# A graph network's edge matrix with a column per node, built from tiles of five nodes; first pass written out

## Reference, cut to what matters

```python
def gin_conv(x, W_a, b_a, W_b, b_b):                     # layer 0, twice
    agg = segment_sum(x[src], dst, N)
    return relu((agg + x) @ W_a + b_a) @ W_b + b_b
...
def gcn(x):                                              # layer 1, two hops
    x = relu(x); deg = segment_sum(1, dst, N); d = rsqrt(max(deg, 1))
    for _ in range(2): x = segment_sum(x[src] * d[src] * d[dst], dst, N)
    return x
...
# layer 2: three spline convolutions (each edge mixes 8 of 64 matrices by its
#   attributes), mean over a node's edges, leaky relu, batch norm
# layer 3: attention with 4 heads over the same edges (softmax by segment)
```

## Time and profile before

| | |
|---|---|
| median of three runs | 13,891.47 us (13,890.89, 13,891.47, 13,902.91) |
| span of the profiled execution | 13,892.9 us (it has no time of its own beside the span) |
| busy PE, PEld | 8,563.9 us (62%), 5,687.6 us (41%) |
| busy DVE, ACT, POOL | 7,277.8 (52%), 2,041.8 (15%), 9,883.4 (71%) |
| setup | 0 to 84.87 us |
| gin1, its node phase | 84.87 to 1,763.59, to 1,909.63 |
| gin2, what stands between | to 3,217.70, to 3,325.42 |
| gcn1, what stands between | to 4,134.10, to 4,184.33 |
| gcn2 | to 4,994.07 |
| spline passes and attention | to 13,892.9 |

### The profile page before, as it was taken

The page is one execution under the profiler, slowest core; times in us unless marked ns, Lnnn a source line. Parts: engine busy times, 40 slices in busy tenths (PEclk is TensorE's granted clock), DMA queues, the critical chain, the costliest instruction groups (busy, mean ns, idle before and its releaser), DMA issues.

```text
span 13892.9 us, 190634 instructions
## 1 busy us (share of the span) xinstructions
PE 8563.9 (62%) x45374; PEld 5687.6 (41%) x45374; DVE 7277.8 (52%) x21844; ACT 2041.8 (15%) x1668; POOL 9883.4 (71%) x10259
## 2 busy tenths in 40 slices
PE   5666667776877866666667666667666660033315
PEld 2333323333444445545445545545455540032305
DVE  5555522223333366666666666666666661245637
ACT  5666710000000001111111111111111110000000
POOL 7777747775767757777767777767777765777772
PEclk8887868888989977778878887778778775566657
DMA  4544523344767730000010000010000002122212
GB/s 122 154 143 145 150 70 102 103 107 115 215 181 215 214 75 13 13 13 13 13 16 13 13 13 13 13 16 13 13 13 13 13 12 38 32 57 57 57 39 47
DMA packets 1111612, 930.87 MB, mean 67 GB/s; under 512 B 312738, under 2 KB 1066308, under 8 KB 1111061
## 3 DMA queue, kind: packets, MB, share of 16 engines
q10 hardware_dynamic: 641040, 670.91, 15.8%
q0 software_dynamic: 325632, 190.97, 8.8%
q1 hardware_dynamic: 144518, 64.66, 2.1%
HBM read 718.69 MB, written 207.12 MB: 67 GB/s over the span
## 4 chain that ended last, share of the span: by engine, by line
POOL 62%; issue 22%; PE 7%; DVE 4%; ACT 2%; DVEq 1%; DMA 1%; ACTq 0%; SPq 0%; POOLq 0%
POOL work L802 62%; PE ps L910 2%; PE ps L925 2%; ACT nodes L1289 2%; DVEq L1740 1%; PE ps L1111 1%; PE ps L898 1%; PE ps L1028 0%; DVE big L1750 0%; DVE big L1823 0%; DVE nodes L1762 0%; PE ps L1122 0%; PE ps L1139 0%; DVE nodes L1758 0%; ACTq L1413 0%
## 5 line engine op out<-in xcount | busy, mean ns | idle before, releaser
L802 POOL DMA_INDIRECT work<-tab_sp,nodes x4992 | 4725.1, 947 | 1735.6 <-issue 1520.1
L1006 PE MATMUL ps<-work 128*128 128x192 f32 x9984 | 2671.8, 411 | 1905.9 <-DVE work L1672 1850.4
L1006 PEld LDWEIGHTS ps<-work 128*128 128x128 f32 x9984 | 1992.9, 232 | 2482.0 <-issue 1440.7
L1921 DVE TENSOR_TENSOR work<-work,ps 128x192 f32 x4992 | 1748.3, 350 | 719.9 <-PE ps L1006 372.6
L802 POOL DMA_INDIRECT work<-tab_att,nodes x1664 | 1603.9, 964 | 628.3 <-issue 628.3
L991 PE MATMUL ps<-work,wk 128*32 128x144 f32 x10080 | 1760.9, 327 | 2.3 <-DVE work L1921 2.3
L925 PE MATMUL ps<-nodes,work 128*96 128x480 fp8e4 (+1 forms) x6664 | 1613.9, 400 | 64.7 <-DVEq L1872 59.2
L802 POOL DMA_INDIRECT work<-in_x,idx x1248 | 1302.8, 1044 | 416.8 <-issue 375.5
L1750 DVE TENSOR_TENSOR big<-big,ps 33x12 f32 (+2 forms) x3520 | 554.8, 158 | 1939.5 <-PE ps L898 1214.5
L1672 DVE TENSOR_TENSOR work<-work,ps 128x512 f32<-128x512 f32 x1248 | 856.0, 686 | 1333.5 <-DMA work<-tab_sp,nodes 1317.9
L1331 ACT ACTIVATE work<-zero 128x2496 f32<-128x2496 f32 x318 | 725.4, 2282 | 5453.1 <-PE ps L991 5448.4
(11 more groups left out here) (241 smaller groups left out, 6117.1 us busy)
## 6 DMA issues: line engine op xcount, KB each, us to landing
nodes<-counts_d ACTq DMA_DIRECT2D x612, 660.0 KB
counts_d<-nodes ACTq DMA_DIRECT2D x130, 1188.0 KB
work<-tab_sp,nodes POOLq DMA_INDIRECT x4992, 2.4
work<-counts_d ACTq DMA_DIRECT2D x117, 528.0 KB
work<-edge_rows SPq DMA_DIRECT2D x112, 320.0 KB
edge_rows<-work ACTq DMA_DIRECT2D x104, 320.0 KB, 2.2
work<-tab_att,nodes POOLq DMA_INDIRECT x1664
work<-in_x,idx POOLq DMA_INDIRECT x1248
```

Source lines behind the costliest of these rows:

```text
L802: pool.indirect_dma_start(out=rows(p, r)[:, t, 0:ROW[p]], out_offset=None, in_=TABLE[p], in_offset=bass.IndirectOffsetOnAxis(ap=place, axi ...
L1006: last = nc.tensor.matmul(moment_place(t), u0[:, s % 2, t % SUB, :], vb[:, t % AHEAD, :, :].rearrange("p k j -> p (k j)"), start=True, sto ...
L1921: v.tensor_tensor(to, to, got, ALU.add).then_inc(mom_added.sem, 1)
```

## The change

The matrix gets a column per node in place of a 12-wide window per tile. Five successive target nodes (KN) are a tile, so a block of counts is 128 x 490 (98 x 5), and the five columns of one tile touch those of the next: a pair of 40 tiles is 200 nodes, 2,000 tiles (KT) in 50 pairs are 10,000 nodes. Where a tile's edges begin isn't known before: in the setup DVE counts, for each of 16 groups of 128 five-node tiles, how many edge tiles begin below its first node; POOL gathers those edge tiles' targets (16 gathers) and, once DVE has counted on, sources and targets of 128 edges a tile (32 gathers); DVE works out codes, an edge that doesn't belong to the five nodes gets a code that matches nothing, PE turns codes and low parts, ACT copies them out. The test now compares 14 neighbours instead of 10, in a ring of 8, and asks that no five nodes have too many edges.

Dense are now the first 9,800, 8,800, 10,000 and 10,000 nodes. Near halves fall to 24, 32, 22 and 22 (384, 512, 352 and 352 gathers); at the seam a 32-tile stretch has its edges to dense nodes hidden while a pass runs (`cut_off`).

In gin1, PE builds two tiles a step, one product of 490 columns each into a PSUM bank of its own (a ring of three steps; the code ring goes from 4 to 8), ACT evicts the two in one instruction of 980 elements, 5 adjacent bytes at a time 200 bytes apart, and the dense product takes the pair's counts straight from the staging buffer, 98 products of 200 columns, while the next pair is built. The store of a whole pair (2.5 MB) is issued by SP. All of gin1 is written out on PE, DVE and ACT, in turns of 80 tiles with one near half each. The later passes are written out as well: units of 400 columns, pieces through a ring of six, 22 units in gin2 and 25 in each gcn pass; DVE adds a finished unit in one instruction at a fixed place. x is turned in the setup beside DVE's counts.

The diff, cut to its core:

```diff
-DT = 1040
-DENSE = {"gin1": 416, "gin2": 640, "gcn1": DT, "gcn2": DT}
-UNIT = {"gin1": 32, "gin2": 40, "gcn1": 40, "gcn2": 40}
-PIECES = {"gin1": 2, "gin2": 2, "gcn1": 3, "gcn2": 3}
+KN = 5
+KSTEP = 2
+PAIR = 40
+PN = PAIR * KN
+PAIRS = 50
...
+NEAR_HALVES = {"gin1": 24, "gin2": 32, "gcn1": 22, "gcn2": 22}
+DENSE = {p: ET - G * n for p, n in NEAR_HALVES.items()}
+DENSE_NODES = {"gin1": 9800, "gin2": 8800, "gcn1": PAIRS * PN, "gcn2": PAIRS * PN}
+UNIT = 2
+UN = UNIT * PN
...
+PIECES = 6
+CODE_RING = 8
...
+DIST = 14
+PAIR_RING = 8
...
+            def store_pairs():
+                with sp.Fori(0, PAIRS // 2) as i:
+                    for h in range(2):
+                        j = 2 * i + h
+                        sp.wait_ge(evicted.sem, evicted.done("gin1", STEPS * j + (STEPS - 1)))
+                        sp.dma_start(counts_d[bass.ds(j, 1), :, :, :].rearrange("g c p n -> p (g c) n"),
+                                     staged_out[:, h, :].rearrange("p (c n) -> p c n", c=NCH)).then_inc(counts_out[h], 16)
...
+            hold(pool, "pool", firsts_known, 1)
+            for c in range(KCOLS):
+                pool.indirect_dma_start(
+                    out=dst_rows[:, c, :], out_offset=None, in_=single_dst,
+                    in_offset=bass.IndirectOffsetOnAxis(ap=tile_edge[:, c:c + 1], axis=0),
+                ).then_inc(dst_rows_in, 16)
+            hold(pool, "pool", edges_known, 2)
+            for c in range(KCOLS):
+                for to, single, at_ in ((edge_src, single_src, first_edge), (edge_dst, single_dst, first_ext)):
+                    pool.indirect_dma_start(
...
-            def build_counts(n, b):
+            def build_counts(n, b, step, ring):
...
-                for q in range(3):
-                    w = CODES // 3
-                    last = nc.tensor.matmul(ps[:, 3 * (b % 2) + q, 0:w], lo_oh[:, (b // SUB) % 2, b % SUB, :],
-                                            code_oh[:, b % 4, q * w:(q + 1) * w], start=True, stop=True)
-                last.then_inc(built.sem, 1)
+                for q in range(KSTEP):
+                    hold(pe, "pe", code_made.sem, code_made.done("gin1", n + q))
+                    if q == 0:
+                        pe.wait_ge(evicted.sem, evicted.done("gin1", step - 3))
+                    nc.tensor.matmul(ps[:, 2 * ring + q, 0:KC], lo_oh[:, (b // SUB) % 2, (b + q) % SUB, :],
+                                     code_oh[:, (b + q) % CODE_RING, :], start=True, stop=True).then_inc(built.sem, 1)
...
+                def dense(j, h, e):
+                    blocks_ = dense_blocks(e)
+                    if e == DENSE_FROM:
+                        hold(pe, "pe", evicted.sem, evicted.done(p, STEPS * j + (STEPS - 1)))
+                        hold(pe, "pe", unit_added.sem, unit_added.done(p, j - 2))
+                        pe.sem_inc(asked_pe, 1)
+                    for t in blocks_:
+                        last = nc.tensor.matmul(ps[0:SPLIT1, 7, 256 * h:256 * h + PN], parts1[:, t, 0:SPLIT1],
+                                                staged_counts[:, h, t * PN:(t + 1) * PN], start=(t == 0),
+                                                stop=(t == NT - 1))
...
+                    for x in range(2):
+                        for e in range(STEPS):
+                            f = STEPS * x + e
+                            build_counts(TURN_K * turn + KSTEP * f, KSTEP * f, 2 * STEPS * turn + f,
+                                         (2 * STEPS * phase + f) % 3)
+                            if k is not None and f in NEAR_AT:
+                                near(k, y, NEAR_AT.index(f), i)
+                            if k is not None or x == 1:
+                                dense(2 * turn + (x - 1), 1 - x, e)
...
+            def evict_counts():
...
+                            if e == 0:
+                                hold(act, "act", counts_out[x], 16 * turn + 16)
+                                hold(act, "act", pair_used.sem, pair_used.done("gin1", 2 * turn + (x - 2)))
+                            act.wait_ge(built.sem, built.done("gin1", TURN_K * turn + (KSTEP * f + KSTEP - 1)))
+                            nc.scalar.activation(out_[:, KSTEP * e:KSTEP * (e + 1), :, :],
+                                                 ps[:, 2 * ring:2 * ring + KSTEP, 0:KC].rearrange("p q (m w) -> p q m w", w=KN),
+                                                 ACT.Copy, saturate=False).then_inc(evicted.sem, 1)
...
+                def add_pair(j, h, n_added):
...
+                    to = acc[0:SPLIT1, bass.ds(j * PN, PN)]
+                    v.tensor_tensor(to, to, ps[0:SPLIT1, 7, 256 * h:256 * h + PN], ALU.add).then_inc(unit_added.sem, 1)
...
+                def add_unit(u, n_added):
...
+                    to = acc[0:m, u * UN:(u + 1) * UN]
+                    v.tensor_tensor(to, to, ps[0:m, u % 4, 0:UN], ALU.add).then_inc(unit_added.sem, 1)
...
+            for c in range(KCOLS):
+                link(v.tensor_scalar(pen_f[:, 0:SEEN], first_target.bitcast(I32)[:, 0:SEEN], group_f[:, c:c + 1], None,
+                                     ALU.is_lt, ALU.add, accum_out=tiles_before[:, c:c + 1]))
...
+            dve.wait_ge(dst_rows_in, 16 * KCOLS)
+            link(v.tensor_tensor(dst_less, dst_rows, by_slot(group_i), ALU.is_lt))
+            link(v.tensor_reduce(in_tile[:, :], dst_less, axis=AX.X, op=ALU.add))
...
+            dve.wait_ge(edges_in, 32 * KCOLS)
+            link(v.tensor_scalar(grid_code, srcs, 1.0 / P, 0.5 / P - 0.5, ALU.mult, ALU.add))
```

More of the change, by code:

```diff
@@ L88 @@
 EPS = 1e-5
-DIST = 10
+DIST = 14
+PAIR_RING = 8
 MOST_CLOSE = 5
-CHECKED = DT * P // ET
+CHECKED = -(-SEEN * P // ET)
+FAR_OFF = 1024.0
 assert ET * P >= E and NT % BT == 0 and BLOCKS % 2 == 0 and ET % P == 0 and HALVES * G == ET
 def ring_of(p, close):
-    return 3 if close and p in ("gin1", "gcn1", "gcn2") else RING
+    return 3 if close and p == "gin1" else RING
 def chunk_halves(q):
@@ L396, in build @@
         counts_out = [sem("counts_out0"), sem("counts_out1")]
-        piece_in = [sem(f"piece_in{r}") for r in range(3)]
+        piece_in = [sem(f"piece_in{r}") for r in range(PIECES)]
         far_known = sem("far_known")
@@ L805, in half @@
                         ).then_inc(quarter_in[r][t // SUB] if p in SPLINE else gathered[p][r], 16)
-                if close and p not in ("gin1", "gin2"):
+                if close and p == "gin1":
+                    hold(pool, "pool", near_idx_in, 16)
+                    for k in range(near_halves(p)):
+                        half(k, k % ring, k // ring, near_idx)
+                    return
+                if close and p != "gin2":
                     hold(pool, "pool", all_src_in, 16)
-                    for k in range(near_halves(p) if near else HALVES):
-                        half(k, k % ring, k // ring, True)
+                    for k in range(near_halves(p)):
+                        half(k, k % ring, k // ring, all_src[:, DENSE[p] if near else 0:])
                     return
@@ L914, in piece_product @@
-            def piece_product(p, c, r, landed, sides):
-                groups = UNIT[p] // OCT
+                    hold(pe, "pe", lo_made.sem, lo_made.done("gin1", n // SUB if isinstance(n, int) else step * KSTEP // SUB))
+                for q in range(KSTEP):
[4 more added lines that the diff above has]
+                                     code_oh[:, (b + q) % CODE_RING, :], start=True, stop=True).then_inc(built.sem, 1)
@@ L1319, in copy_turned_rows @@
+            def load_counts(p):
+                for c in range(UNITS[p] * NCH):
+                    (u, ch), r = divmod(c, NCH), c % PIECES
+                    hold(act, "act", piece_used.sem, piece_used.done(p, c - PIECES))
+                    act.dma_start(landing(r), counts_d[UNIT * u:UNIT * (u + 1), ch, :, :]
+                                  .rearrange("g p n -> p g n")).then_inc(piece_in[r], 16)
             def copy_turned_rows(p):
@@ L1409, in _ @@
             nc.scalar.activation(warm[:, :], work[:, C:C + 1], ACT.Copy)
-            turn("x")
+            act.wait_ge(consts, 9)
+            for b in range(BLOCKS):
+                act.wait_ge(turned_ps.sem, turned_ps.done("x", b))
+                nc.scalar.activation(acc[0:C, b * BN:(b + 1) * BN], flat(2 * (b % 2), BN, C), ACT.Copy).then_inc(turned.sem, 1)
             act.wait_ge(rw_clear, 1)
@@ L1826, in near_pass @@
+                near_one_hots(p, 0, 0)
+                turn_(0)
+                for k in range(near_halves(p)):
+                    turn_(k + 1, k, k % 3)
+                add_pair(UNITS[p] - 1, (UNITS[p] - 1) % 2, added.events(p))
             def near_pass(p):
-                hpt, steps = near_plan(p)
-                turns = NEAR_TURNS[p]
-                def add_octs(unit, u, octs, n_added):
+                def add_unit(u, n_added):
+                    m = P if p == "gin2" else 3 * C
```

584 lines of the change are left out of this document (281 added, 303 removed).

## The result

The changed kernel takes 12,222.07 us, the median of four runs (12,217.25 to 12,223.42), for 13,891.99 of the kernel before, measured beside it: 0.8797 of it, 95% interval 0.8785 to 0.881. The forecast was 12,365 in a range of 12,200 to 12,620. The profiled execution spans 12,219.7 us.

What follows compares the result with a forecast made beforehand. POOL's gathers were taken to bound each linear pass. Against the 13,892.9 us before, setup +65, gin1 -509, node phase +8, gin2 -458, gcn1 -317 and gcn2 -318 gave 12,365, range 12,200 to 12,620.

Steps and rivals of the forecast that it cites:

- its ends (1,090 to 1,360): The lowest and highest time in us that the prediction allowed for the gin1 pass, around its 1,170.
- DVE's pair: DVE's work in gin1 for one pair of 40 tiles, put at 21.4 us and taken as the slowest engine's.
- the rival of the short runs: gin1: evictions writing 5 bytes, then jumping 200, cost 1.15 us, the pass 1,255, the total 12,450; chance 0.11.
- the copy of 128 elements: Strided copy at 0.449 us where the slope gives 0.28, read as 1.3 ns a jump for gin1's evictions.
- the 7% of idle time: gin1: the bounding engine idles 0.61 us per 8.53 in an earlier stretch, so 21.4 a pair became 23.
- the forecast's sign: gin1: DVE busy over 85% of the pass was listed among what would show the forecast right.
- The rival that PE and DVE hinder each other: gin1: with dense products at 0.177 us the pair takes 26.8, the pass 1,360, the total 12,555; chance 0.14.
- the half clock of its start: gin2: PE starts the pass at half clock, which raised its 835 us to 850.
- Three near-equal limits: gcn1 and gcn2: PE 473, loads 473 and POOL 440 us, with a six-piece ring, gave 492 a pass.
- The rival that DMA starves PE: Slower loads and half-clock waits make each gcn pass 560 us and gin2 900, the total 12,550; chance 0.08.
- the rival that would have ended on the other side: Four written-out passes: PE's instruction stream 40 ns late per instruction, 1,536 us, gives 13,900; slower had chance 0.04.
- all overlaps fully: Case with gin1 1,090, setup 125 and gcn 475 us, the total 12,225; chance 0.05.

## Why the prediction came out as it did

**Bound before, and the gathers' price: right.** Taking gathers away was worth what separates POOL from the next engine, pass by pass. The run with 8,800 nodes shows it from the other side: gcn with 512 gathers is POOL's again, at 1.26 each.

**gin1: wrong in the engine, and within its ends (1,090 to 1,360) by luck.** Three steps failed. DVE's pair was put at 21.4 and needs 18.2. The one-hots were a little cheaper (0.26 for 0.28, 0.16 for 0.18), and the window adds were priced by a row in which each waits for the one before (0.26); between one-hots they cost 0.07, so eight cost 0.6 for 2.1. The pair add took 0.27 by the timeline's next start, for 0.45. The second step is the eviction: 0.89 was right for adjacent writes (0.87) and wrong for these (1.10), 22 a pair for 17.9. That is the rival of the short runs, in its price (1.15) and place; its trigger, a cost per jump, is not, since runs 10 bytes apart cost nothing extra. Its price was luck too: the copy of 128 elements that it was read from hops in what it reads and writes runs of 16, and hops of the reads cost nothing here. The third is the 7% of idle time added to the bounding engine, 80 us over the pass, with 20 for filling and draining: ACT waits 11.3 us once, at the start, and no more. 22.0 x 50 is 1,100, which is the pass; 23 x 50 and 20 for filling was 1,170. The two errors of price largely cancelled (21.4 and 22.0 a pair, 30 us), and idle time and filling less these 30 made the difference of 68. DVE was busy for 941 of the 1,102 us, 85%, as the forecast's sign asked, with ACT as the bound: that sign could not tell the two engines apart.

The Trainium skill, Vector Engine (DVE) Microarchitecture Reference, section "Measured stream behaviour on trn2", says that a port streams at full rate only over runs of at least two adjacent 4-byte words that start on an 8-byte boundary. For ACT's writes the runs agree in kind: runs of 5 cost 1.10, runs of 10 0.93, adjacent bytes 0.87, and the price comes back every fourth step. They don't agree in size: the factor of 1.62 from that section's figures, taken over to ACT, gave an estimate of 1.45 an eviction, where the runs show 1.10, and 0.87 for runs of 5 that fill each other's gaps.

**Dense products: 0.095 forecast, 0.086 measured;** the lower end was 0.083. The rival that PE and DVE hinder each other falls with it, and the code ring's depth makes no difference.

**gin2: right.** PE bounds at 831 for 835 before the half clock of its start was added. The clock stands at 0.97 in the first 90 us, so most of those 15 us were not lost. The product was put at 0.179 and takes 0.180 from row to row.

**gcn: the mechanism right, the size off by 31 a pass.** Three near-equal limits were put at 473, 473 and 440 and rounded up to 492. PE's own was 460 (0.173 a product for 0.179, 0.35 a near group for 0.4), and the ring of six hides the loads behind it completely: PE idles 2 us in 460 with the DMA engines 91% busy. The rival that DMA starves PE is what happens with three places, 539. So two terms failed: the allowance of 19 above the slowest limit, which was worth nothing, and 13 in PE's limit itself.

**Setup: +72 for +65.** The counts took 26.5 for 24, and the edge gathers and their landing took 46 for 42. The wait of 4.85 for POOL's stretched gathers is the 5 that the forecast allowed for them. DVE's timeline no longer holds the turning of x, as costed.

**Instruction supply:** the rival that would have ended on the other side is void. In gin2, written out, PE is busy for 829 of 831 us. The Trainium skill, Runtime: NRT & Kernel Launch, section "Instruction fetch mechanics", says that the cost of fetching on in sequence is mostly hidden; the trace agrees.

The whole time, 12,222, lies below the forecast's own range (12,260 to 12,470, chance 0.58) and 22 us above the lower end of the wide one. The nearest case was that all overlaps fully (12,225, chance 0.05), and that the sum came so near to it is luck: gin1 took 12 more than its 1,090 and the setup 32 more than its 125, while each gcn pass took 14 less than its 475 and gin2 19 less than 850.

## What to carry to other kernels

Once the slowest engine's work is cut, the next bound is read from rows of a stretch where that engine doesn't wait, and each row must fit the way the new code uses it: a chain of adds that wait for each other prices a chain, not an add between other work, and an eviction's slope is that of its runs. An output pattern is worth trying in both orders of its inner loops: here one reordering of the same elements, 10 bytes in a run for 5, gave 170 us. Where PE and DMA are nearly equal, the depth of the load ring decides which of them shows, and the allowance above the slower limit can be none.

## What the runs showed of the hardware that was not expected

- ACT's writes of fp8: 980 elements from PSUM took 0.87 us to adjacent bytes, 0.87 in runs of 5 whose gaps the same instruction fills, 0.93 in runs of 10 that stand 200 apart, 1.07 in runs of 5 that stand 40 apart, 1.10 at 200 apart; 784 elements in runs of 4 took 1.01. The last four are means over steps, which go from 0.88 to 0.98, 1.00 to 1.11, 1.00 to 1.15 and 0.83 to 1.12 and come back every fourth step, that is, every 40 bytes. What the place costs by itself stays open.
- Reads that change between two PSUM banks every five columns cost ACT nothing extra: gin1 1,971.5 us for 1,971.4.
- ACT's records overlap when its writes are slow: records of 2.15 us at 1.10 us from one to the next, where those to adjacent bytes are 1.02 us long at 0.91.
- POOL's gathers are stretched beside long DVE operations: 1.50 us each while the comparisons ran, 0.94 once they had ended.
